# Attention over 16 images on one core: TensorE's side work dealt out as single matmuls on both sides of the value product, and turned maxima moved into the row-maximum banks

## What is computed

```python
# x: (16, 512, 32, 32) float32; 8 heads of 64; T = 1024 tokens of C = 512
def _gn(v, G=32, eps=1e-5):            # mean and variance over each group of channels
    ...
    return ((g - m) / jnp.sqrt(s + eps)).reshape(v.shape)

xs = reshape(_gn(x), (B, T, C))        # a plain reshape, no transpose
q = einsum('btc,hcd->bhtd', xs, Wq)    # and k, v likewise
scores = einsum('bhtd,bhsd->bhts', q, k) / 8
att = softmax(scores, axis=-1)
out = einsum('bhts,bhsd->bhtd', att, v) # heads side by side
return x + (out @ Wproj + bproj)       # reshaped back
```

## Time and profile before

| | |
|---|---|
| time, median of 3 runs | 4906.41 us (4905.99 to 4906.59) |
| the profiled execution | 4906.69 us, span of its instructions 4904.9 us |
| TensorE (PE) busy | 4571.5 us, 93% of the span, 20,864 matmuls |
| ScalarE, VectorE, GpSimd busy | 60%, 57%, 51% |
| DMA engines busy | 15.2% |
| mean granted TensorE clock | 0.989 of full speed |

### The profile page before, as it was taken

The page is one execution under the profiler, slowest core; times in us unless marked ns, Lnnn a source line. Parts: engine busy times, 40 slices in busy tenths (PEclk is TensorE's granted clock), DMA queues, the critical chain, the costliest instruction groups (busy, mean ns, idle before and its releaser), DMA issues.

```text
span 4904.9 us, 74324 instructions
## 1 busy us (share of the span) xinstructions
PE 4571.5 (93%) x20864; PEld 3615.4 (74%) x20864; DVE 2778.6 (57%) x5286; ACT 2929.7 (60%) x5637; POOL 2485.3 (51%) x1965
## 2 busy tenths in 40 slices
PE   7999999999999999999999899999999999999998
PEld 5777777777777777777777777777777777777776
DVE  5655646556465564655646556465564655646554
ACT  4665746556465564655646556565665656657465
POOL 2455545455454454545545545455455554455456
PEclk9999999999999999999999999999999999999999
DMA  2111111111111111111111111111112111121111
GB/s 69 35 41 52 31 54 36 44 49 30 54 35 48 44 35 51 36 51 41 34 53 32 56 38 33 54 35 51 41 30 61 31 53 38 30 64 33 51 26 52
DMA packets 156935, 212.72 MB, mean 43 GB/s; under 512 B 56544, under 2 KB 57568, under 8 KB 156512
## 3 DMA queue, kind: packets, MB, share of 16 engines
q1 hardware_dynamic: 156512, 207.47, 15.2%
HBM read 105.12 MB, written 34.08 MB: 28 GB/s over the span
## 4 chain that ended last, share of the span: by engine, by line
issue 49%; POOL 44%; PE 5%; POOLq 1%; ACT 1%; DVE 1%; DMA 0%; SPq 0%; ACTq 0%; DVEq 0%
POOL prob_l L1043 32%; POOL o L1063 6%; POOL o_l L1072 2%; POOL xs L1077 2%; PE bank L508 2%; POOL rstd L1035 1%; POOLq L1042 1%; PE bank L570 1%; PE bank L681 1%; PE bank L683 0%; PE bank L682 0%; PE bank L564 0%; PE bank L563 0%; ACT prob_h L700 0%; ACT prob L700 0%
## 5 line engine op out<-in xcount | busy, mean ns | idle before, releaser
L1043 POOL TENSOR_TENSOR prob_l<-prob,prob_h 128x512 fp32r<-128x512 f32 x1408 | 1804.1, 1291 | 2289.4 <-ACT prob_h L700 2280.2
L700 ACT ACTIVATE prob<-bank 128x512 f32<-128x512 f32 x2048 | 1238.4, 605 | 1627.7 <-PE bank L564 1468.7
L871 DVE TENSOR_REDUCE smax<-bank 128x1 f32<-128x512 f32 x2048 | 1347.7, 683 | 956.9 <-PE bank L570 944.9
L700 ACT ACTIVATE prob_h<-bank 128x512 fp32r<-128x512 f32 x2048 | 1237.4, 604 | 193.3 <-PE bank L683 156.7
L681 PE MATMUL bank<-prob_h,vh 128*128 128x512 f32 x2048 | 835.6, 408 | 111.4 <-ACT acc L785 100.4
L563 PE MATMUL bank<-q_hh,k_hl 128*128 128x512 f32 x2048 | 818.4, 400 | 13.0 <-issue 12.5
L564 PE MATMUL bank<-q_lm,k_h 65*128 65x512 f32 x2048 | 813.5, 397 | 0.0
L683 PE MATMUL bank<-prob_l,vh 128*128 128x512 f32 x2048 | 811.0, 396 | 0.0
L682 PE MATMUL bank<-prob_h,vl 128*128 128x512 f32 x2048 | 810.9, 396 | 0.0
L810 DVE TENSOR_TENSOR prob_l<-prob,prob_h 128x512 fp32r<-128x512 f32 x640 | 510.0, 806 | 500.0 <-ACT prob_h L700 499.4
L570 PE MATMUL bank<-k_hl,q_hh 128*128 128x512 f32 x2048 | 757.3, 414 | 34.1 <-DVE smax L871 30.8
(11 more groups left out here) (68 smaller groups left out, 5149.8 us busy)
## 6 DMA issues: line engine op xcount, KB each, us to landing
xs<-in_x SPq DMA_DIRECT2D x256, 256.0 KB, 2.7
q_hh<-q_hh SPq DMA_DIRECT2D x256, 128.0 KB, 2.2
k_hl<-k_h SPq DMA_DIRECT2D x256, 128.0 KB, 2.3
inv_b<-inv_dram SPq DMA_DIRECT2D x256, 128.0 KB, 2.8
out_x<-xs SPq DMA_DIRECT2D x128, 256.0 KB, 2.0
q_lm<-q_lm SPq DMA_DIRECT2D x256, 2.0 KB
den<-acc SPq DMA_DIRECT2D x256, 2.0 KB, 1.7
inv_dram<-inv SPq DMA_DIRECT2D x256, 2.0 KB, 1.4
```

Source lines behind the costliest of these rows:

```text
L700: return nc.scalar.activation(out, ps[ST + bank][:, :], ACT.Exp, scale=SCALE)
L871: nc.vector.tensor_reduce(smax[:, j:j + 1], ps[SM + j % 2][:, :], AX.X, ALU.max).then_inc(rows_used, 1)
L1043: nc.gpsimd.tensor_tensor(prob_l[:, r3, :], prob[:, ring2, :], prob_h[:, r3, :].bitcast(F32), ALU.subtract).then_inc(prob_l_pool, 1)
```

## The change

The tables `WORK`, `MAXIMA` and `FIRST` become one table. For each kind and slot it has two lists, the work ahead of the value product (side 0) and that behind it (side 1); each item names the kind, the entry and *how many single matmuls* of it are issued there, `row` and `mt` among them. An entry may so be spread over up to eight slots.

```diff
-CHUNKS = {"qk": 4, "qn": 4, "v": 4, "xt": 4, "proj": 4, "mean": 1, "var": 1, "mt": 1}
+UNITS = {"qk": 12, "qn": 12, "v": 24, "xt": 4, "proj": 12, "mean": 1, "var": 1}
 WORK = {
-    "plain": ((1, "mt", 1, 0, 1), (10, "mt", 0, 0, 1), (10, "qn", 0, 0, 3), (12, "qn", 1, 0, 3),
...
+    "plain": (
+        ((("qn", 0, 4),), (("qn", 0, 1), ("mt", 1, 1))),
...
+    "proj": (
+        ((), ()),
+        ((("row", 0, 1),), (("row", 0, 1),)),
...
-FIRST = {
-    "plain": ((0, 8), (), (0, 7, 14)),
...
+PROJ_SLOTS = tuple(slot for slot, sides in enumerate(WORK["proj"]) for kind, a, n in sides[0] + sides[1] if kind == "proj" and n == 12)
+CAST_SLOTS = (0, 1, 2, 3, 6, 7, 8, 9)
+SPLIT_SLOTS = tuple(slot + 1 for slot in CAST_SLOTS)
+
+LATE = {"plain": (0, 7, 14), "tokens": (8,), "next": (6, 13, 14)}
...
+TAKE_QN = 13
-MEAN_SLOTS = (5, 8)
+MEAN_SLOTS = (5, 9)
```

A work bank goes to the entry that comes first once it is free, no longer in strict turn; `taken` is counted for each bank:

```diff
-                            assert len(ends) < 2 or ends[-2] < s
-                            ends.append(BLOCKS)
+                            bank = ended.index(min(ended))
+                            assert ended[bank] < s - (side == 0)
...
+                        if hi == UNITS[kind]:
+                            taken = max(s + 1, TAKE_QN if kind == "qn" else 0)
```

`mt` leaves the work banks: it takes its turn with `row` in the two SM banks, and a `row` or `mt` waits for whoever used its bank two turns ago, a reduction or a copy. The order of the row products changes so that the first four need the first half of the keys alone:

```diff
+def row_of(j):
+    group, j = divmod(j, 8)
+    half, t = divmod(j, 4)
+    return 4 * group + t, half
...
-                nc.vector.tensor_copy(mrow[:, half, :], ps[WB + bank][0:4, 0:P]).then_inc(taken[bank], 1)
+                nc.vector.tensor_copy(mrow[:, half, :], ps[SM + turn][0:4, 0:P]).then_inc(mt_used, 1)
...
+                            if j in (0, 4):
+                                half = j // 4
+                                pe.wait_ge(k_split, s.heads(2, 1, half + 1))
...
+                            _, _, bank, user = s.turn("row", j)
+                            turn_free(s, user)
```

More of the change, by code:

```diff
@@ L131, in __init__ @@
-                slots = fillers(k % 8, has_next, k == 8)
-                assert not slots[BLOCKS - 1]
-                ends = []
+                slots = fillers(k % 8, section != "last", k == 8)
+                ended, holder, takes = [-2, -1], [None, None], [[] for _ in range(BLOCKS)]
                 for s, slot in enumerate(slots):
-                    for kind, a, lo, hi in slot:
+                    for side, kind, a, lo, hi in slot:
+                        if kind in ("row", "mt"):
+                            continue
@@ L149, in __init__ @@
+                self.steps[section, k], self.takes[section, k] = slots, takes
             if section == "body":
-                self.per_batch = n - body_start
+                self.per_batch = [used[b] - body_start[b] for b in range(2)]
         for t in range(8):
-            self.place["last", 8, ("proj", t)] = n + t
-        assert self.per_batch % 2 == 0
+            self.place["last", 8, ("proj", t)] = (t % 2, used[t % 2] + t // 2)
 class Step:
@@ L164, in __init__ @@
         self.slots = plan.steps.get((section, k))
-        self.first = FIRST[step_kind(self.h, self.has_next, section == "body" and k == 8)]
+        self.takes = plan.takes.get((section, k))
         self.looped = section == "body"
         self.proj = self.looped and k == 8
+        self.late = LATE.get(step_kind(self.h, self.has_next, self.proj), ())
         self.rows_slots = EARLY_ROWS if self.proj else ROWS_SLOTS
         self.out_slots = EARLY_OUT if self.proj else OUT_SLOTS
+        self.turns, user = [], [None, None]
+        for kind, a in [(e[1], e[2]) for slot in self.slots or [] for e in slot if e[1] in ("row", "mt")]:
+            n = sum(e[0] == "row" for e in self.turns)
+            bank = len(self.turns) % 2
+            self.turns.append((kind, n if kind == "row" else a, bank, user[bank]))
+            user[bank] = (kind, n if kind == "row" else a)
     def at(self, per_batch, const):
@@ L299, in attention_block @@
         mt_done = sem("mt_done")
+        mt_used = sem("mt_used")
         proj_done = sem("proj_done")
@@ L755, in step @@
                     ahead, j = divmod(i + AHEAD, BLOCKS)
-                    late = i in s.first[2]
+                    late = i in s.late
                     if late:
-                        for kind, a in s.done(i):
+                        for kind, a in s.takes[i]:
                             take_in_step(s, kind, a)
```

426 lines of the change are left out of this document (275 added, 151 removed), and 10 rows, old and new, of the table WORK.

## The result

| | before | after |
|---|---|---|
| time, median of 4 runs each | 4906.5 us (4905.99 to 4908.46) | 4650.44 us (4645.54 to 4651.7) |
| ratio, 95% interval | | 0.9476 (0.9459 to 0.9492) |
| TensorE busy | 93% | 97% |
| mean granted clock | 0.989 | 0.994 |

The change makes the kernel 256 us (5.2%) faster. Predicted were 323 us.

What follows compares the result with a forecast made beforehand. TensorE, busy 93%, was taken as the bound. Savings of 9.1 us (projection) and 12.1 (plain parts) make 21.2 a round, 318 us in 15 rounds, plus 5 outside: 4907 - 323 = 4584 us, range 4535 to 4730.

Steps and rivals of the forecast that it cites:

- The bound and the way to count: Whole kernel: TensorE sets the end, 93% busy; step lengths less matmuls at dense spacing give 36.2 us lost a round.
- k1: First step of a round, a values step: side work ahead of the value product saves 1.2 us; listed at 34.5 us.
- The start-up: Before the loop: the turned maxima wait for all 16 reductions, about 1 us lost, once.
- The projection step: Last step of a round: earlier casts and splits shorten the waits for `o_l`; 9.1 of 12.1 us saved.
- Cover in slots 0 and 8: Side work ahead of the value product hides the copy of PVB: 0.55 us plus up to 0.4 of lateness each.
- k4: Fourth step of a round, a plain one: 1.2 us saved, to 28.1 us.
- Tokens: Sixth step of a round: 2.4 us saved, 3.3 of 5.7 lost kept, with slots 9 to 11 crowded.
- The 85%: Plain parts of a round, 14.2 us saved in small covers: only 85% taken, 12.1, since short slots leave less slack.
- Rival B: Waits move into the 25 short slots a round without a side matmul other than `mt`: about 4710 us; chance 0.22.
- Rival C: Each turned maximum in the row banks holds TensorE for VectorE, 2.1 us x 240: 5088 us; chance 0.07.
- Rival D: Proj step: waits move from one projection to the next and cancel the gain, within 10 us of 4906; chance 0.05.
- Single matmuls at no cost: Entries issued as single matmuls cost nothing; bound 1 us a step, 120 us in the loop if never hidden.

Runs made afterwards that it cites:

- late casts: Changed kernel with casts two slots and splits one slot ahead of each projection, as before the change: 4811.08 us, ratio 0.9808.
- copy first: Changed kernel with ScalarE's copy of PVB ahead of the exponential, in the slot before the proj step: 4652.36 us, ratio 0.9487.
- without cover: Changed kernel with all side work of slots 0 and 8 behind the value product again: 4683.12 us, ratio 0.9551.
- old order: Changed kernel's banks and start-up with the work table, casts and splits of the kernel before: 5013.2 us, ratio 1.0217.
- mean later: Changed kernel plus block 3 on GpSimd, bare round start, early variance and tokens' row cover (4616.69 us), then tokens' mean and what follows a slot later: 4667.63 us.

## Why the prediction was right, and where it was off

**The bound and the way to count.** Right. TensorE stayed the bound (97%), and the loop of 15 rounds fell from 4556.3 to 4301.3 us: 255 of the 261 us by which the two spans differ, 17.0 a round. (The table's means give 16.6; they leave out the first round, in which k1 has no stall.) The other 6 us lie outside the loop, where I gave 5. The start-up is 3.8 us longer up to the first score product of a step (74.6 to 78.4), not 1; the runs with the same start-up show 76.5 to 79.3, and at the start of the loop 0.5 us of it is left in this trace.

**The projection step.** Mechanism right: 8.1 us of the 9.1. The table gives TensorE 32.9 us of dense work in slots 1 to 10, not the 33.3 that I set against GpSimd's 31.3; nothing hung on it. One part of the loss I had not seen: in the kernel before the clock falls not only behind the wait of 2.85 us, in all 15 rounds, but also behind that of 1.79 us in slot 0, in ten of them, and the proj steps of these ten take 62.1 us where the other five take 61.1. The round of the earlier trace rows is one of the five. In the changed kernel no proj step of the loop has a lower clock. The `o_l` waits fell to 10.5 us (forecast: under 30), and the late casts show what the order of GpSimd is worth. Off is slot 0: I wrote that the two casts moved behind the copy take "1.2 us" off its wait of 1.79. The wait became 1.27, 0.5 less. In the changed kernel ScalarE starts the copy 1.17 us into the step with the casts behind it; two exponentials stand ahead, one of them held by a value product. And had it been sized rightly, the first projection would not have come earlier by it, as the run with the copy first shows.

**Cover in slots 0 and 8.** The wait for `acc` fell to 22.2 us as forecast (under 30). "Each is worth what it covers: 0.55 plus up to 0.4 of lateness" was too much: without cover it costs 0.39 where ScalarE is in time, and the covers are worth 33 us in all. The wait fell by 34 us without cover (100.4 to 66.6) and by 44 with it, of which 33 reached the time. In k1 the worth of cover hardly shows, since the stall of the loop's edge grows by what the cover saves. For k2, k5 and next the sums held nonetheless (33.8, 28.4, 46.7 for 33.7, 28.1, 46.7).

**k1.** The saving of 1.2 us for the first values step did not come. The earlier trace rows gave it 3.3 us of loss against 2.2 for the second, the same work, and I took the difference for a wait that cover could hide. In the loop's first round that was so: there TensorE waits 1.16 us for the copy of PVB before and not at all now, and the step goes from 35.53 to 33.83 us, 1.7 saved. In the 14 others the stall behind the jump stands in that place. It was 0.9 us behind the value product and is 1.9 us in front of it, and these steps went from 35.84 to 36.55 us. The term that I had left out is the stall; it keeps 2.7 us a round from the step (36.55 against 33.83), 38 us in all. Against the sum, k1 misses 26 us. The list of steps that I gave also says 34.5 for k1, which is 1.8 saved and not 1.2, and it adds up to 280.6 us where the sum of 21.2 saved gives 282.3.

**k4.** "I put plain at 1.2 and 2.0 saved": k5 gained 1.5, k4 lost 0.5. I had followed TensorE and ScalarE in this step, and not VectorE, which in k4, and not in k5, also normalises input at the start of the step, and whose `prob_l` stretches beside GpSimd's. One `prob_l` given to GpSimd brought k4 to 28.4. The miss of 1.7 a round is 25 us.

**Tokens.** "I keep 3.3 of 5.7": 29.3 - 24.6 = 4.7 are kept. The largest wait is in slot 9, 1.06 us on average and 1.52 us in six rounds of 15. In three rounds the clock falls behind it (0.94 in the step), which I had counted only for proj; these steps take 30.5 us, and the shortest without it 28.5. Two attempts moved or shortened this wait and gained nothing; what would stays open. 18 us.

**The 85%.** I took off 15% of the plain parts for covers that spoil each other. Over all 15 rounds the steps saved 17.0 us a round, 6.3 short of the full 23.3: 95 us (k1 26, k4 25, tokens 18, proj 14, the rest 12). The allowance covered 32 of them and the steps outside the loop brought 1 more than forecast, which leaves 62 us, and 62 is what lies between the forecast and the profiled run (4645.5); the median is 5 us above it. The misses are not spread evenly, as a percentage would have it; three places hold 69 of the 95. That the time fell within the range owes something to an allowance that was made for another reason.

**Rival B, short slots.** Didn't happen. Bare slots 10, 11, 14 and 15 of the plain steps lose 0.03 us each or less, and TensorE's wait for GpSimd's `prob_l` is 4.3 us in all. The time lies between my forecast's and B's, but for other reasons.

**Rival C, the maxima as a wait.** Its mechanism is real, its place count was not. In the changed kernel it costs 16.2 us, 13.2 of them in k4, where each round waits 0.88 us although 15 matmuls, 3.4 us of dense work, stand between the `mt` and the row that wants its bank: that distance was the wrong measure, since VectorE and not TensorE was late. With the old order it is 102 us in 62 waits of 1.65 us, above the 1.35 us from which I said it decides, but in a quarter of the 240 places; that kernel is slower than the one before, and how much of it these waits make was not run apart. The sign that I gave for this rival, `smax` as TensorE's longest wait, came true without it: `smax` now heads the list with 29.4 us because the others fell, and it was 30.8 before. A sign should have named a size. The Trainium skill ("Perfetto Trace Analysis", Matmuls), which wants one bank emptied while the next is filled, holds in both: the table decides whether the bank is empty in time.

**Rival D.** Fell: the projection waits went, and came back nowhere. (I gave it a chance of 0.05 and the class "same" 0.02, though it would have been within 10 us of none; the two do not agree.)

**Single matmuls at no cost.** Held: from the value product to `qn` (1643.11 to 1643.35 in the timeline) the next matmul starts after 0.24 us, and between two `qn` after 0.23.

## What to carry to other kernels

On an engine that issues in order, look for the instruction that stands ahead of a wanted one and is itself wanted later: asking for five of the eight small splits one or two slots earlier was worth 161 us, all cover by side work 33. Before filling or moving a wait, follow the engine that releases it (here VectorE) as closely as the one that waits; where that engine is late by itself, the wait only changes its name. A step that loses more than its twin has a cause of its own, which should be found before a saving is booked on it; the first round of a loop, which no jump precedes, is a free experiment on the loop's edge.

## What the runs showed of the hardware

VectorE's groups in the changed kernel (busy us, mean ns, idle before):

```profile
L1024 DVE TENSOR_REDUCE smax<-bank 128x1 f32<-128x512 f32 x2048 | 1347.8, 682 | 431.4 <-PE bank L706 425.4
L962 DVE TENSOR_TENSOR prob_l<-prob,prob_h 128x512 fp32r<-128x512 f32 x640 | 576.2, 904 | 607.0 <-ACT prob_h L852 606.9
L991 DVE TENSOR_SCALAR xs<-xs,gmean,rstd 128x512 f32<-128x512 f32 x128 | 106.5, 864 | 2.3 <-POOL rstd L1178 2.3
```

- The same 640 subtractions took 806 ns before and 904 after, the same 128 normalisations 552 and 864, the reductions 683 and 682. Alone, a `prob_l` takes 0.69 us in both kernels; the 182 before and 286 after that overlap a GpSimd instruction take 1.10 and 1.17 on average, up to 1.79. In the new order their work falls together more often, and VectorE's busy time grew by 88 us. The Trainium skill ("SBUF — State Buffer", Who interferes with whom) says that a VectorE instruction with two inputs in SBUF contends with GpSimd's reads, and a reduction never does; the trace agrees. In the row at 1643.14 the `prob_l` ends 0.54 us after GpSimd's, which began first. The normalisations, which have one large input, slowed as well, 0.54 us alone and 1.00 beside GpSimd on average.
- Behind the loop's jump back, TensorE stands still once a round after five matmuls, for 0.5 to 1.3 us in the kernel before and 1.6 to 2.3 in the changed one, and goes on 1.1 to 1.6 us after a 16 KB transfer of instructions has landed. None of the runs removed it.
- The length of a single gap does not tell whether the clock falls. Behind 1.79 us (proj's slot 0, before) it fell in ten rounds of 15, behind 2.47 us (first projection, before) in none of five, behind 2.85 us in 15 of 15, behind 1.52 us (tokens, changed kernel) in three of six, behind 1.71 us (mean later) in 13 of 15. The wait of 1.79 us in a round with a fall and in one without, before:

```profile
351.20:355.70 4.50, 4.25 (x12) 3.28 (x13) 3.56 (x7) 2.88 (x7) 1.76 (x2) 0.62 0.48 137
1870.90:1875.40 4.50, 4.47 (x20) 3.58 (x21) 4.38 (x7) 3.70 (x8) 2.59 (x3) 1.00 0.47 127
```
